# Beginning the gates' transposes, store and first broadcast loads beside the twelfth key tile

## The reference

```python
scores = softmax(xt @ router_w + router_b) + router_bias      # 16 routed experts in 4 groups
keep   = the 2 best groups; idx = the 2 best experts in them; gate[t, idx] = scores[t, idx]
for each expert: y += gate[:, e, None] * ((silu(xt @ w1 + b1) * (xt @ w2 + b2)) @ w3 + b3)
y += (silu(xt @ sw1 + sb1) * (xt @ sw2 + sb2)) @ sw3 + sb3    # shared, run as two more experts
...
k = rmsnorm(ctx @ k_proj_w.T)      # second layer, 8 heads of 128; needs the context alone
```

## Time and profile before

| | us |
|---|---|
| median of 3 executions | 688.44 (688.21 to 688.82) |
| profiled execution | 687.87 |
| its span, first to last instruction | 686.1 |
| TensorE busy in the span | 630.3 (92%) |
| VectorE / ScalarE / GpSimd busy | 435.5 / 346.1 / 326.9 |
| mean granted TensorE clock | 0.970 |
| DMA queue 1 (SyncE's) / queue 10 (ScalarE's), share of 16 engines | 55.3% / 2.4% |

### The profile page before, as it was taken

How to read it: one execution, slowest core, us unless ns; L and a number is a source line. 1 busy time by engine, 2 the same in 40 slices (tenths; PEclk the granted TensorE clock), 3 DMA queues, 4 the chain that set the end, 5 groups by cost and what they waited for, 6 DMA issues and landing times.

```text
span 686.1 us, 11191 instructions
## 1 busy us (share of the span) xinstructions
PE 630.3 (92%) x3004; PEld 281.0 (41%) x3004; DVE 435.5 (63%) x991; ACT 346.1 (50%) x754; POOL 326.9 (48%) x310
## 2 busy tenths in 40 slices
PE   5729989889999999999998599999999979999997
PEld 2314534334444444444443134444444424444453
DVE  5999887354334443855555899999999950000673
ACT  4514535333334333476676677777777743143132
POOL 4923134255445552177878444444444433458111
PEclk9958999899999999999999999999999999999999
DMA  8802035444453433158794999999999995315001
GB/s 330 361 0 76 10 77 93 102 125 138 147 141 123 131 99 123 62 124 218 163 215 92 222 175 188 174 181 182 185 182 182 182 185 158 120 65 183 1 1 62
DMA packets 200314, 95.65 MB, mean 139 GB/s; under 512 B 187962, under 2 KB 188090, under 8 KB 197341
## 3 DMA queue, kind: packets, MB, share of 16 engines
q1 hardware_dynamic: 197490, 90.49, 55.3%
q10 hardware_dynamic: 2795, 4.79, 2.4%
HBM read 48.03 MB, written 1.09 MB: 72 GB/s over the span
## 4 chain that ended last, share of the span: by engine, by line
PE 60%; DVE 18%; issue 8%; POOL 7%; SPq 3%; ACT 2%; DMA 1%; DVEq 0%; POOLq 0%; ACTq 0%
PE ps L276 20%; PE ps L277 19%; PE ps L278 19%; POOL wsp L1042 4%; POOL hlr L1042 3%; SPq L367 3%; DVE st L1165 1%; DVE nw L1177 1%; DVE nw L1176 1%; DVE f32r L1181 1%; DMA stage<-in_first_chunks 1%; DVE xT L1240 1%; PE ps L615 1%; DVE v_sb L1217 1%; DVE nw L1178 1%
## 5 line engine op out<-in xcount | busy, mean ns | idle before, releaser
L1042 POOL TENSOR_TENSOR wsp<-stage,wsp 128x512 f16<-128x512 f32 (+1 forms) x93 | 134.5, 1470 | 140.3 <-ACT wsp L775 72.5
L920 ACT ACTIVATE f32r<-f32r,mneg 128x512 f32<-128x512 f32 x128 | 91.4, 715 | 29.7 <-DVE mneg L1404 29.7
L1042 POOL TENSOR_TENSOR hlr<-f32r,hlr 128x512 f16<-128x512 f32 x52 | 60.8, 1179 | 90.1 <-ACT hlr L828 56.4
L1404 DVE CUSTOM_DVE_ANT_0 f32r<-ps,nmask 128x512 f32<-128x512 f32 x128 | 82.4, 679 | 1.9
L1122 POOL TENSOR_SCALAR stage<-f32r,rinv 128x512 f16<-128x512 f32 x64 | 44.2, 704 | 46.3 <-DVE rinv L1409 46.3
L1122 POOL TENSOR_SCALAR hlr<-f32r,rinv 128x512 f16<-128x512 f32 x64 | 43.6, 695 | 47.0 <-DVE rinv L1409 45.4
L1323 DVE TENSOR_REDUCE ss<-f32r 128x4 f32<-128x512 f32 x48 | 32.9, 685 | 44.0 <-ACT f32r L816 43.9
L276 PE MATMUL ps<-k_sb,q_sb 128*128 (+1 forms) x128 | 48.8, 381 | 11.7 <-DVE mneg L1404 9.1
L276 PE MATMUL ps<-q_sb 128*128 128x512 f16 x128 | 50.1, 391 | 10.2 <-POOL q_sb L1042 7.4
L1373 DVE SCALAR_TENSOR_TENSOR f32r<-ps,par,f32r 128x512 f32<-128x512 f32 x18 | 13.5, 750 | 72.2 <-PE ps L278 71.6
L276 PE MATMUL ps<-xT,wsp 128*128 128x512 f16 x144 | 55.9, 388 | 2.6 <-DVE stage L1365 2.6
(11 more groups left out here) (231 smaller groups left out, 1350.4 us busy)
## 6 DMA issues: line engine op xcount, KB each, us to landing
stage<-in_moe SPq DMA_DIRECT2D x18, 512.0 KB, 3.7
stage<-in_wq SPq DMA_DIRECT2D x8, 1024.0 KB, 5.2
stage<-in_wo SPq DMA_DIRECT2D x8, 1024.0 KB, 5.1
stage<-in_moe SPq DMA_DIRECT2D x18, 256.0 KB, 3.3
hlr<-gates_dram ACTq DMA_DIRECT2D x18, 256.0 KB, 3.2
k_sb<-in_wkv SPq DMA_DIRECT2D x3, 1024.0 KB, 18.5
stage<-in_first_chunks SPq DMA_DIRECT2D x4, 512.0 KB, 5.4
q_sb<-in_ctx_nat SPq DMA_DIRECT2D x1, 2048.0 KB, 14.8
```

The source lines that it names most:

```text
L920: act.activation(f32r[:, j % 4, :], f32r[:, j % 4, :], ACT.Exp, bias=mneg[:, j % 4:j % 4 + 1], scale=-1.0, accum_out=psum_col[:, j % 4:j % ...
L1042: return pool.tensor_tensor(dst_lo, src, dst_hi, ALU.subtract)
L1404: dve.tensor_tensor_reduce(f32r[:, j % 4, :], ps[j % 4][:, :], nmask[:, qt, :], 0.125, BIG, ALU.add, ALU.min, mneg[:, j % 4:j % 4 + 1]).th ...
```

## The change

The gates' transposes go before key tile 11 on TensorE, VectorE's copy before its part of tile 11, ScalarE's store and cast behind its part of tile 11 (the store first). The first two broadcast loads go to SyncE, between the transposes of tile 14 and those of tile 15, behind a wait for the store. `gate_bc` moves from `hlr` to `pT2`, which is used only later, and ScalarE's waits for `s_gst`, `s_kT[2]` and `s_kT[3]` go. The second round of the key phase is written out on TensorE, ScalarE and VectorE instead of a loop.

```diff
-        gate_bc = [hlr[:, 2, :, :].rearrange("p a b -> p (a b)").bitcast(F32),
-                   hlr[:, 3, :, :].rearrange("p a b -> p (a b)").bitcast(F32)]
+        gate_bc = [pT2[:, n, :, :].rearrange("p a b -> p (a b)").bitcast(F32) for n in range(2)]
...
             for r in range(2 * NST):
                 k_transpose(r)
+                if r == 14:
+                    sp.wait_ge(s_gst, 16)
+                    for n in range(2):
+                        sp.dma_start(gate_bc[n], gates_dram[n:n + 1, :].partition_broadcast(P)
+                                     .rearrange("q a t -> q (a t)")).then_inc(s_gload[n], 16)
...
-            def first_expert():
+            def gate_transposes():
                 pe.wait_ge(s_gate, 1)
                 for t in range(NT):
                     last = pe.transpose(ps[5][0:NE, t * P:(t + 1) * P], gt[:, t, :], identf)
                 last.then_inc(s_gT, 1)
-                up(0, 0, (0,))
...
-            rms_phase(0, 2, 8, k_project, lambda: pe.wait_ge(s_vfree, NST + 4))
-            first_expert()
-
+            def beside_keys(r):
+                if r == 8:
+                    pe.wait_ge(s_vfree, NST + 4)
+                if r == 11:
+                    gate_transposes()
+
+            rms_phase(0, 2, 8, k_project, beside_keys)
+            up(0, 0, (0,))
             pe.wait_ge(s_gTc, 1)
             up(0, 0, (1,))
...
+            def gates_split():
+                act.wait_ge(s_gTc, 1)
+                act.dma_start(gates_dram, gateT[0:NE, :]).then_inc(s_gst, 16)
+                act.copy(gatesT[0], gateT[0:E_ROUTED + 1, :]).then_inc(s_gh, 1)
...
-            rms_phase(0, 2, 8, 1.0 / HD, scs[:, 12:13], s_kT, 32)
+            rms_phase(0, 2, 8, 1.0 / HD, scs[:, 12:13], s_kT, 32, None, {11: gates_split})
...
-            act.wait_ge(s_gTc, 1)
-            act.copy(gatesT[0], gateT[0:E_ROUTED + 1, :]).then_inc(s_gh, 1)
-            act.dma_start(gates_dram, gateT[0:NE, :]).then_inc(s_gst, 16)
-            act.wait_ge(s_gst, 16)
-            for s in range(2):
-                act.wait_ge(s_kT[2 + s], 16 * NST)
-                gate_load(s, s)
             for s in range(2):
                 act.wait_ge(s_kT[s], 16 * NST)
                 expert(s, s)
...
+            def gates_turned():
+                dve.wait_ge(s_gT, 1)
+                dve.tensor_copy(gateT[0:NE, :], ps[5][0:NE, :]).then_inc(s_gTc, 1)
...
-            rms_phase(0, 2, 8, True, gates)
+            rms_phase(0, 2, 8, True, {4: gates, 11: gates_turned})
...
-            dve.wait_ge(s_gT, 1)
-            dve.tensor_copy(gateT[0:NE, :], ps[5][0:NE, :]).then_inc(s_gTc, 1)
             dve.wait_ge(s_gh, 1)
             dve.tensor_tensor(gatesT[1], gateT[0:E_ROUTED + 1, :], gatesT[0], ALU.subtract).then_inc(s_gl, 1)
```

More of the change, by code:

```diff
@@ L427, in v_rows, with rms_phase @@
                     last.then_inc(s_vp, 1)
-            def rms_phase(r0, iters, tiles, project, after_first=None):
+            def rms_phase(r0, iters, tiles, project, beside=None):
                 def body(i, first):
@@ L433, in body @@
                         r = r0 + tiles * i + j
+                        if beside:
+                            beside(r)
                         if not first or j >= 4:
@@ L438, in rms_phase @@
                 body(0, True)
[L439 to L442, removed]
+                if beside:
+                    for i in range(1, iters):
+                        body(i, False)
+                else:
+                    with pe.Fori(1, iters) as i:
+                        body(i, False)
             def k_project(i, j):
@@ L808, in _, with rms_phase @@
             act.activation(sml[:, 4:8, :], sml[:, 0:4, :], ACT.Exp).then_inc(s_rex, 1)
-            def rms_phase(r0, iters, tiles, scale, bias, s_T, landed, quarter=None):
+            def gates_split():
+                act.wait_ge(s_gTc, 1)
+                act.dma_start(gates_dram, gateT[0:NE, :]).then_inc(s_gst, 16)
+                act.copy(gatesT[0], gateT[0:E_ROUTED + 1, :]).then_inc(s_gh, 1)
+            def rms_phase(r0, iters, tiles, scale, bias, s_T, landed, quarter=None, beside=None):
                 def squares(r, j, first):
@@ L840, in body @@
                                 quarter(i, j // 4, c)
+                        if beside and r in beside:
+                            beside[r]()
                 body(0, True)
-                with act.Fori(1, iters) as i:
-                    body(i, False)
+                if beside:
+                    for i in range(1, iters):
+                        body(i, False)
+                else:
+                    with act.Fori(1, iters) as i:
+                        body(i, False)
                 end = tiles * iters
@@ L1346, in body @@
                         r = r0 + tiles * i + j
-                        if first and j == 4 and beside:
-                            beside()
+                        if beside and r in beside:
+                            beside[r]()
                         sums(r, j, first)
@@ L1353, in rms_phase @@
                 body(0, True)
-                with dve.Fori(1, iters) as i:
-                    body(i, False)
+                if beside:
+                    for i in range(1, iters):
+                        body(i, False)
+                else:
+                    with dve.Fori(1, iters) as i:
+                        body(i, False)
                 normed(r0 + tiles * iters - 1, tiles - 1, False)
-            rms_phase(0, 2, 8, True, gates)
+            rms_phase(0, 2, 8, True, {4: gates, 11: gates_turned})
             dve.wait_ge(s_mask, 16)
             dve.tensor_scalar(nmask[:, :, :], nmask[:, :, :], -8.0, None, ALU.mult).then_inc(s_ol, 4)
-            dve.wait_ge(s_gT, 1)
-            dve.tensor_copy(gateT[0:NE, :], ps[5][0:NE, :]).then_inc(s_gTc, 1)
             dve.wait_ge(s_gh, 1)
```

## The result

| | before | changed |
|---|---|---|
| median, us | 688.44 (688.21 to 688.82) | 681.33 (678.78 to 682.17) |
| ratio, 95% interval | | 0.9890 (0.9862 to 0.9918) |
| profiled execution / its span | 687.87 / 686.1 | 681.91 / 680.2 |
| first matmul of the first expert to that of the third | 26.26 | 20.67 |

The changed kernel is 7.1 us faster in the median, 8.2 were forecast. I call the stretch of the last line the seam: it is where the change acts. As in the code, experts are counted from 0: the first is expert 0, the second expert 1. Its profile gained 5.6 us there and 5.9 in the span.

What follows compares the result with a forecast made beforehand. TensorE's 72 matmuls between key projection and third expert took 26.26 us for 15.5, through waits and half clock. Savings 2.2 + 1.8 + 2.5 + 1.7 = 8.2 us gave a median of 680.2, range 678.4 to 683.0 for 8 in 10.

Steps and rivals of the forecast that it cites:

- the terms 2.5 (wait) and 1.7 (its half clock): At the first down products: TensorE's 2.5 us wait for hidden rows and 1.7 us of half clock behind it both go.
- the low part of the gates: VectorE's step ahead of the bias products: taken as 0.68 us, done by 125.24, leaving TensorE 0.66 us idle.
- the term 2.2 us: Ahead of the bias products: TensorE's idle falls from 2.8 to 0.66 us, saving 2.2 us.
- the half clock behind the bias run: In expert 1's matmuls after the gate-bias matmuls: slow clock left as it was, at 1.7 us.
- my signs of being wrong: Loads taking over 4.2 us, TensorE's clock falling in other places, or holes in the expert loop.
- The late hidden rows: Rival at the down products: hidden rows hold TensorE 1.05 to 1.3 us, giving 681.3 to 683.2; chance 0.22.
- the slack of 0.55 us: At the down products: hidden rows ready at 134.25, 0.55 us before TensorE wants them at 134.8.
- The ring order: On SyncE's queue: descriptors are consumed in order, so gate loads would stand behind the transposes; size not shown.
- my upper bound: Gate loads on SyncE: starting only once the transpose of 127.10 has landed, they land at 133.6 instead of 132.0.
- Other half clock: Rival: more or less half clock than counted, giving 679.6, 678.5 or 681.9; chance 0.17.
- The stretch behind 558.77: Late half clock behind a 2.77 us idle, priced at 1.7 us; it might fall away, giving 678.5.
- its written-out loops: Slower rival: written-out key loops cause instruction fetches in later loops, 3.0 us slower, 691.4; chance 0.02.

Runs made afterwards that it cites:

- e4: Kernel before, with only the spread gates moved to the unused tile and ScalarE's waits for tiles 14 and 15 removed: 683.87 us, ratio 0.9919.
- e1: The changed kernel measured again without any edit: 680.58 us, ratio 0.988.
- e3: Changed kernel with spread gates back in the key slots and ScalarE issuing the loads after waiting for tiles 14 and 15: 688.87 us, ratio 1.0004.
- e7: Changed kernel with the two gate loads issued by ScalarE behind its last key tile instead of by SyncE: 680.28 us, ratio 0.9873.
- e9: The changed kernel measured a third time without any edit, on another chip: 682.63 us, ratio 0.9894.
- e11: Changed kernel with SyncE's gate loads behind tile 12's transposes instead of tile 14's: 683.44 us, ratio 0.9918.
- e2: Changed kernel with VectorE's low part of the gates moved ahead of key tile 12's sums: 680.83 us, ratio 0.9882.
- e5: Changed kernel with the four bias products spread through expert 1's matmuls instead of one run ahead of them: 681.67 us, ratio 0.9893.
- e10: Changed kernel with low part early, bias products spread and loads behind tile 12, in its second measurement: 678.36 us, ratio 0.9844.
- e8: Changed kernel with the gates' low part early and SyncE's gate loads behind tile 12's transposes: 679.8 us, ratio 0.9865.

## Why the prediction was right

**Right, with sizes.** The key phase is unhurt: keys end at 119.45 (119.40 forecast), the copy lies in VectorE's idle, and ScalarE still idles 0.79 us ahead of tile 12's squares, so not even the 0.13 us were paid; the store's issue ran beside the squares, at 109.47 instead of 110.5. It had landed long before SyncE asked. The load landed after 3.6 us as taken; it went out 0.35 us later than forecast. The gate product took 0.69, the hidden rows were ready at 134.42 (134.25 forecast), and the down products came straight behind expert 1's matmuls. So the terms 2.5 (wait) and 1.7 (its half clock) were gained whole, and e4 isolates them: 4.3 us of seam.

**Mis-sized: the low part of the gates.** I priced it at 0.68 and the idle at 0.66. It took 1.63, the idle is 1.54 (1.55 in e1, e3, e7, e9 and e11). The cause is shown, not only argued: the instruction ends 0.55 us behind GpSimd's split, and takes 0.67 where e2 moves it away from that split. I had weighed this very rule of the Trainium skill ("SBUF — State Buffer", who interferes with whom) for the gate product alone. What fails is the step "0.68 like the copy that leaves this place": the copy reads PSUM and took 0.67 at 124.08, beside GpSimd's split of 122.45 to 125.16; the low part reads two SBUF operands. Of the term 2.2 us 1.1 stay.

**Mis-sized: the half clock behind the bias run.** I left it at 1.7 us. From the bias products to the down products it is 7.88 us at full clock (125.11 to 132.99 in e2, where the wait of 1.83 us is not counted), 9.51 to 9.56 in e1, e7 and e11, so 1.65, and 11.2 in the first profile and in e9, so 3.3: there it began within the bias run and lasted through the first 10 or 13 of expert 1's matmuls. "If TensorE's clock falls in other places" stood among my signs of being wrong: it did, and the sum stayed within the range all the same. Forecast seam 18.0; with the low part 19.1, which is what e1, e7 and e11 show (19.0), and with the second stretch 20.7.

**Read wrong: the key phase.** "Up to 119.4 us TensorE has no hole and runs at full clock" holds from 98.00 only, where the earlier trace rows begin. Ahead of it the kernel before waits 2.80 us, until 93.96, and runs at half clock behind it:

```profile
93.96 0.39 PE L276 MATMUL ps<-q_sb 128*128 128x512 f16 x1 [2.80 <-DVE f32r L1336]
...
94.53 0.63 PE L278 MATMUL ps<-q_sb 128*128 128x512 f16 x1
```

No term of the sum rests on this, but it hid one more place where an execution wins or loses 1.7 us (column k).

**The rivals.** The late hidden rows did not decide in the changed kernel. They came as forecast (134.42), and TensorE came later than forecast (137.53 for 134.8), so the slack of 0.55 us was never tried. Where TensorE comes earlier, by an early low part and full clock (e2) or by spread bias products and a short k (e5), they hold it for 1.83 or 2.74 us. The ring order of the Trainium skill ("DMA: Bandwidth & Descriptors", Queues, rings and completion order), named beside my upper bound, did not show: the profiles have 3.6 to 4.1 us to landing behind transposes on SyncE's queue, 3.4 to 4.2 on ScalarE's (e7). Other half clock: it happened both ways, in the seam (20.7 against 19.0) and behind the attention loop (121.6 against 123.3). The stretch behind 558.77 was mispriced at 1.7: in the first profile of the changed kernel it is gone, and the two late waits end 5.68 us apart for 5.70 before, as the second wait grew from 1.21 to 2.72. I gave other half clock 0.17 as a case of its own; it is rather the spread of every execution, some 5 us from the fastest to the slowest of the changed kernel in one measurement. That the change costs by its written-out loops: e3 has them and the ratio is 1.0004.

**Why the median comes near all the same.** Sum of the seam as corrected: 26.26 less 19.0 to 20.7, so 5.6 to 7.3 us, and up to 1.7 us either way at k and at the end. The three medians of the changed kernel lie 7.1, 8.0 and 6.1 below the kernel before. The forecast of 8.2 stands at the upper end, by the 1.1 us of the low part. How near a single median came is in part luck: the three gains lie 1.9 us apart, and the sum has no term for that spread.

**Open.** Why the same code gets 7 or 15 half-clock matmuls in the seam, and why in e2 the bias run brings none. The same holds for k and the end, where the same waits were followed by a half clock or not. The runs show only what stands before, idles of 1.5 us or more or seventeen-row matmuls in one run, and none of it brings a half clock every time. That the gain of e10 is due to its full clock in the seam and not to the idles alone is likely from the seams (16.37 twice, no half clock twice, against one in e8, which has no idle either), but two profiles are few.

## What to carry to other kernels

Where two chains meet at an engine, price both arrivals: of two waits removed here, one alone was worth 4.7 us, the other alone nothing, and the second paid only once the first was gone. When an instruction moves next to another engine's work, ask for each of its operands where it lies: VectorE with two SBUF operands beside GpSimd took 1.63 us for 0.67. Before comparing two profiles, take out the stretches ahead of and behind the edit: here each of the two moved the span by up to 1.7 us. Spreading the seventeen-row matmuls between wide ones is not shown to pay by itself: alone it brought nothing in time (e5), and on top of the two other edits 0.4 us in the median (679.43 against 679.8), within the noise.

## What the runs showed of the hardware that I had not expected

- A kernel whose waits are equal to 0.01 us from execution to execution had seams of 19.0 or 20.7 us, by TensorE's granted clock alone; the wait of 2.80 us at 94 us was followed by a half clock in ten profiles and by none in three. Single times of the changed kernel lay up to 5.2 us apart.
- A run of twelve seventeen-row matmuls without any idle before it was followed by eight matmuls at half clock in e8, and by none in e2.
- A half clock can be free: ahead of the second late wait it shortens that wait from 2.7 us to 0.9 to 1.4 (e1, e7, e10, e11); behind it such a stretch costs 1.6 to 1.7.
- Two broadcast loads of 256 KB held SyncE's queue for 1.05 us, against 0.86 to 0.88 for the same two on ScalarE's.
